# A step of four columns: from the turnings of the probabilities to the evictions of the keys

## The chip, the cores and the metric

The kernel runs on one core of a Trainium2 chip. The metric is the device time of one execution in microseconds, the median of several runs. The engines are TensorE (PE in the profile; PEld is its weight load), VectorE (DVE), ScalarE (ACT), GpSimd (POOL) and SyncE (SP), which here issues all DMAs.

## The reference, cut to what matters

32 graphs of 512 nodes with 512 features pass through two layers that share one adjacency matrix. The first is a graph attention with one head; the second is an attention with eight heads of 64 columns. Each layer adds its input and normalises.

```python
x = _layernorm(x + _L0_gnn_ref(x, adj, W, a))      # e = leaky(self + neighbour); masked softmax; alpha @ h; concat h
x = _layernorm(x + _L1_gnn_ref(x, adj, Wq, ...))
# inside the second:
scores = einsum('bhqd,bhkd->bhqk', q, k) / 8       # 512 x 512 for each of 8 heads
scores = where(adj == 0, -inf, scores)
attn = softmax(scores, axis=-1)
out = einsum('bhqk,bhkd->bhqd', attn, v)
```

## The kernel before

All of it is float32, and each matmul operand is split into a high and a low part (HI and LO, both float32r); a product is the sum of three matmuls (or two for the probabilities). The high part is written by ScalarE as a copy from PSUM, the low part by VectorE as the difference of PSUM and the high part, or by GpSimd where the source lies in SBUF.

Work is pipelined over graphs. One round handles the second attention of graph k, the first attention and the projections of graph k+1, and the loads of graph k+2. For each engine a plan (TENSOR_PLAN, SCALAR_PLAN, VECTOR_PLAN, GPSIMD_PLAN, SP_PLAN) writes out by hand in which order its pieces of a round are issued; engines meet at semaphores only, and each works in the order of its plan. The last graph has plans of its own, and a prologue comes ahead of the first.

The second attention of a graph has 32 steps s, one for each pair of a head and a tile of 128 queries:

- TensorE multiplies q and k of a pair of heads into one of four banks S_bank (line 791). Before that, q and k of the pair (two heads, 128 rows, 512 tokens) are evicted from R_bank into qk_pair with the bias added: high parts on ScalarE (line 848), low parts on VectorE (line 999), for q first and then for k, four pairs per graph.
- VectorE adds the mask to the scores while it writes them into prob (three slots) and takes the row extremum (reduce_scores, line 1082). The mask is bf16, 128 rows by 512 columns for each of four tiles.
- ScalarE takes the exponential in place, with the row sum (line 924).
- VectorE turns prob in blocks of 32 by 32 into blocked (turn_blocks, line 1102). The key of column c*128 + i*4 + d has to land in row i*4 + d of block column c later on, and so the turning reads the tile with a step of four columns: for a fixed c and d, 32 columns i that lie four apart.
- Four turned steps go to a scratch in HBM and come back with keys on the rows (scratch, then turned_lo_prob), as one store and one load.
- ScalarE makes the high part (line 838), GpSimd the low part (line 1161), and TensorE weighs v with both into O_bank (line 810).

The first attention of a graph runs its 512 by 512 coefficients through alpha, one tile of 128 rows at a time: ScalarE writes them (line 881), VectorE adds the mask and reduces in place (line 1027, four per graph), ScalarE takes the exponential, and TensorE turns alpha by transposes. Its columns are in the order of the nodes. The same mask serves both attentions.

The mask is built once at the start: adj is loaded into tokens[2], VectorE turns it into 0 or a huge negative number (line 1141), and SyncE waits for that (mask_built) before it loads WqT into the same place.

Of the kernel before, what the change touches and what calls it, by code (L numbers as in the profile page):

```python
# [21 lines left out]
ALU = mybir.AluOpType  # L22
ACT = mybir.ActivationFunctionType
F32 = mybir.dt.float32
F32R = mybir.dt.float32r
BF16 = mybir.dt.bfloat16
I32 = mybir.dt.int32

P = 128
BLK = 32  # L30
# [3 lines left out]
MASKED = -3.0e38  # L34
HUGE = 3.0e38
HI, LO = 0, 1
# [359 lines left out]
def graph_layers(nc, x, xT, adj, W, a, WqT, bq, WkT, bk, WvT, bv, WoT, bo, out):  # L396
    B, N, D = x.shape
    F1 = W.shape[1]
    T = N // P
# [8 lines left out]
    with ExitStack() as ctx:  # L408
# [6 lines left out]
        def sem(name):  # L415
# [8 lines left out]
        mask = sb("mask", [P, T, N], BF16)  # L424
# [5 lines left out]
        tokens = [sb(f"tokens{i}", [P, T, D]) for i in range(3)]  # L430
# [6 lines left out]
        a_negmax, a_sum, a_rsum = a_cols[:, 0, :], a_cols[:, 1, :], a_cols[:, 2, :]  # L437
# [5 lines left out]
        qk_pair = sb("qk_pair", [P, 4, N], F32R)  # L443
# [31 lines left out]
        ident_built, mask_built = sem("ident_built"), sem("mask_built")  # L475
# [7 lines left out]
        a_pre, a_red, a_exp, a_inv = sem("a_pre"), sem("a_red"), sem("a_exp"), sem("a_inv")  # L483
# [4 lines left out]
        qk_hi = sem("qk_hi")  # L488
        v_hi = sem("v_hi")
        s_mm, s_red, p_exp, p_inv, p_turned = (sem("s_mm"), sem("s_red"), sem("p_exp"), sem("p_inv"),  # L490
                                               sem("p_turned"))
# [13 lines left out]
        prologue = Round(0, -1, FIRST_LAYER, last=False)  # L505
        end = Round(0, B, END, more=False, load=False)

        def pair_bank(R, kind, pair):

            if (kind, pair) == ("q", 1):  # L510
                return R_bank[1 - R.bank("k1")]
            return R_bank[R.bank(f"{kind}{pair}")]
# [69 lines left out]
        def prob_tile(R, s):  # L582

            return prob[:, slot_of(R, s), :]
# [17 lines left out]
        def _(sp):  # L602
# [74 lines left out]
                load_tokens(start, i)  # L677
            for j, w in enumerate((WqT, WkT, WvT, WoT)):
                if j == 0:
                    sp.wait_ge(mask_built, 2)  # L680
                else:
                    sp.wait_ge(w_lo, j)
                place = tokens[2][:, :, :] if j % 2 == 0 else stage().rearrange("p (c n) -> p c n", c=C)
                sp.dma_start(place, w.rearrange("(c p) n -> p c n", p=P)).then_inc(w_loaded[1 + j], 16)
                if j == 1:
                    for i in range(T):
                        load_turned(prologue, i)
# [148 lines left out]
        def _(act):  # L836
# [3 lines left out]
            def qk_of_pair_hi(R, pair):  # L840

                if due(R.n(32, 8 * pair)):
                    act.wait_ge(s_mm, R.n(32, 8 * pair))
                for kind, b_col, dst in (("q", bq_col, 0), ("k", bk_col, 2)):

                    ring_mm_value = R.ring("k1") if (kind, pair) == ("q", 1) else R.ring(f"{kind}{pair}", 1)
                    act.wait_ge(ring_mm, ring_mm_value)
                    act.activation(qk_pair[:, dst + HI, :], pair_bank(R, kind, pair)[:, :], ACT.Identity,
                                   bias=b_col[:, pair % 4:pair % 4 + 1]).then_inc(qk_hi, 1)

            def layer_apply(R, which, ahead, i, done):
                t_ap = tokens[R.buffer(ahead)][:, i, :]
# [126 lines left out]
        def _(dve):  # L979
# [16 lines left out]
            def qk_of_pair_lo(R, pair):  # L996
                for j, (kind, b_col, dst) in enumerate((("q", bq_col, 0), ("k", bk_col, 2))):
                    dve.wait_ge(qk_hi, R.n(8, 2 * pair + j + 1))
                    dve.scalar_tensor_tensor(out=qk_pair[:, dst + LO, :], in0=pair_bank(R, kind, pair)[:, :],  # L999
                                             scalar=b_col[:, pair % 4:pair % 4 + 1],  # L1000
                                             in1=qk_pair[:, dst + HI, :].bitcast(F32), op0=ALU.add,
                                             op1=ALU.subtract).then_inc(ring_done, 1)

            def solo_hi_count(R, name):
# [4 lines left out]
            def piece(R, kind, i):  # L1009
# [14 lines left out]
                if kind == "red":  # L1024
                    al = alpha_of(R, i)
                    dve.wait_ge(a_pre, R.nx(4, i + 1))
                    dve.tensor_tensor_reduce(al, al, mask[:, i, :], -1.0, HUGE, ALU.add, ALU.min,  # L1027
                                             a_negmax[:, i:i + 1]).then_inc(a_red, 1)
                if kind == "evD":
                    out_name, t_ap = f"D{i}", tokens[R.buffer(1)][:, i, 0:F1]  # L1030
                    dve.wait_ge(a_inv, R.nx(4, i + 1))
# [63 lines left out]
            def turn_blocks(R, s):  # L1095
                ph = s // 4
                if s % 4 == 0 and due(R.n(8, ph - 1)):
                    dve.wait_ge(*stored(R, ph - 2))
                if s % 4 == 3 and due(R.n(16, 2 * ph - 2)):
                    dve.wait_ge(pv_mm, R.n(16, 2 * ph - 2))  # L1100
                dve.wait_ge(p_exp, R.n(32, s + 1))
                dve.transpose(blocked[:, ph % 2, :, :, 2 * (s % 2) + s % 4 // 2, :].rearrange("p d c i -> p c d i"),  # L1102
                              prob_tile(R, s).rearrange("p (c i d) -> p c d i", c=T, i=BLK)).then_inc(p_turned, 1)

            def half_sum(R, u):
                for w in range(2):
# [25 lines left out]
            for j in range(2):  # L1132
                for c in range(C):
                    if j + c > 0:
# [3 lines left out]
            dve.wait_ge(w_hi, 1)  # L1138
            split_lo(w0[:, LO, :, :], w_stage(), w0[:, HI, :, :], w_lo)
            dve.wait_ge(adj_loaded, 16)  # L1140
            dve.tensor_scalar(mask[:, :, :], tokens[2][:, :, :].bitcast(I32), 0.0, MASKED, ALU.is_equal,
                              ALU.mult).then_inc(mask_built, 1)
            dve.wait_ge(small_loaded, SMALL)
            run_round(start, [START])
            run_round(prologue, [PROLOGUE])
# [108 lines left out]
```

## Time and profile before

| what | value |
|---|---|
| median of 3 runs | 3222.71 us (3222.53 to 3223.19) |
| the profiled execution | 3226.84 us |
| its span, first to last instruction | 3225.0 us |
| mean granted TensorE clock | 0.987 |
| busy: TensorE, VectorE, ScalarE, GpSimd | 3002.1, 2969.1, 2460.1, 2020.8 us |

The span leaves out 1.84 us of the profiled execution's time. Busy time is the union of an engine's instructions; TensorE's matmuls are pipelined, and the ends of their records are modelled. A wait is put down to the semaphore that came last. The granted clock is a share of 2.4 GHz.

### The profile page before, as it was taken

How to read it: one execution, taken by the hardware profiler on the slowest of the kernel's cores; microseconds unless marked ns; L12 is line 12 of the kernel's file. 1: busy time of each engine (PE TensorE's matmuls, PEld its weight loads, DVE VectorE, ACT ScalarE, POOL GpSimd, SP SyncE). 2: the span in 40 equal slices, each digit the busy share in tenths (PEclk: the TensorE clock that was granted, in tenths of full speed). 3: DMA queues.
4: the chain of work that ended last, by engine and by line, in shares of the span. 5: the costliest groups of instructions: out<-in, count | busy, mean ns of one | idle time of the engine just before them, and what ended most of it. 6: DMA issues, size and time to landing. Idle time of an engine off the chain costs nothing.

```text
span 3225.0 us, 58281 instructions
## 1 busy us (share of the span) xinstructions
PE 3002.1 (93%) x19084; PEld 2506.7 (78%) x19084; DVE 2969.1 (92%) x6553; ACT 2460.1 (76%) x5031; POOL 2020.8 (63%) x1415
## 2 busy tenths in 40 slices
PE   5899999999999999999999999999999999999985
PEld 4787788777887787887787887887787877787874
DVE  4999999999999999999999999999999999999985
ACT  3777787777787777877777877777887777877764
POOL 1566666666666666666666666666666666666664
PEclk7999999999999999999999999999999999999998
DMA  3566666665665666666666666666666666666554
GB/s 121 193 211 215 222 235 213 215 210 207 235 226 210 214 214 216 225 233 210 214 213 219 224 228 210 215 215 214 223 230 212 215 213 219 225 217 214 203 199 154
DMA packets 306413, 685.39 MB, mean 213 GB/s; under 512 B 56896, under 2 KB 90432, under 8 KB 273344
## 3 DMA queue, kind: packets, MB, share of 16 engines
q1 hardware_dynamic: 306112, 681.68, 61.8%
q8 instruction: 153, 2.51, 0.3%
q14 instruction: 148, 1.21, 0.1%
HBM read 375.40 MB, written 306.18 MB: 211 GB/s over the span
## 4 chain that ended last, share of the span: by engine, by line
DVE 52%; PE 19%; issue 13%; ACT 7%; DMA 4%; POOL 2%; SPq 1%; DVEq 0%; ACTq 0%; POOLq 0%
DVE blocked L1102 22%; PE R_bank L721 11%; DVE prob L1082 8%; DVE stats L985 4%; DVE alpha L1027 4%; PE O_bank L810 4%; DVE qk_pair L999 3%; DVE o_half L1110 3%; PE S_bank L791 2%; ACT prob L924 2%; DVE tokens L1070 1%; PE L_bank L712 1%; DMA turned_lo_prob<-scratch 1%; DMA r_scratch<-r_cols 1%; ACT turned_hi_prob L838 1%
## 5 line engine op out<-in xcount | busy, mean ns | idle before, releaser
L1161 POOL TENSOR_TENSOR turned_lo_prob<-turned_lo_prob,turned_hi_prob 128x1024 fp32r<-128x1024 f32 x512 | 1237.3, 2433 | 587.3 <-ACT turned_hi_prob L838 585.9
L1102 DVE STREAM_TRANSPOSE blocked<-prob 128x512 f32<-128x512 f32 x1024 | 1102.3, 1099 | 42.6 <-ACT prob L924 30.9
L924 ACT ACTIVATE prob<-prob,small_cols 128x512 f32<-128x512 f32 x1024 | 736.0, 720 | 311.3 <-DVE small_cols L1082 305.4
L1082 DVE CUSTOM_DVE_ANT_0 prob<-S_bank,mask 128x512 f32<-128x512 f32 x1024 | 677.7, 681 | 6.9 <-PE S_bank L791 2.3
L810 PE MATMUL O_bank<-turned_hi_prob,v_st 128*128 128x256 f32 x2048 | 522.8, 292 | 70.2 <-POOL turned_lo_prob L1161 67.2
L838 ACT ACTIVATE turned_hi_prob<-turned_lo_prob 128x1024 fp32r<-128x1024 f32 x512 | 529.0, 1052 | 58.2 <-PE O_bank L810 32.9
L810 PE MATMUL O_bank<-turned_lo_prob,v_st 128*128 128x256 f32 x2048 | 508.3, 285 | 0.0
L810 PEld LDWEIGHTS O_bank<-turned_hi_prob,v_st 128*128 128x128 f32 x2048 | 394.6, 193 | 116.3 <-POOL turned_lo_prob L1161 99.8
L791 PE MATMUL S_bank<-qk_pair 64*128 64x512 f32 x3072 | 448.8, 417 | 31.8 <-DVE qk_pair L999 22.0
L721 PE MATMUL R_bank<-wv,x1T 128*128 128x256 f32 x3072 | 409.6, 287 | 2.2 <-DVE v_st L981 0.2
L721 PEld LDWEIGHTS R_bank<-wv,x1T 128*128 128x128 f32 x3072 | 380.6, 190 | 32.0 <-issue 23.0
L810 PEld LDWEIGHTS O_bank<-turned_lo_prob,v_st 128*128 128x128 f32 x2048 | 395.4, 193 | 4.1
L721 PE MATMUL R_bank<-x1T,wq 128*128 128x512 f32 x1536 | 385.3, 399 | 14.3 <-DVE v_st L981 14.3
L721 PE MATMUL R_bank<-wo,oT 128*128 128x512 f32 x1536 | 387.4, 401 | 2.9 <-POOL oT L1175 1.4
L721 PE MATMUL R_bank<-x1T,wk 128*128 128x512 f32 x1536 | 380.1, 396 | 0.2 <-DVE v_st L981 0.2
L791 PEld LDWEIGHTS S_bank<-qk_pair 64*128 64x128 f32 x3072 | 264.2, 186 | 142.3 <-DVE small_cols L1082 49.4
L721 PEld LDWEIGHTS R_bank<-x1T,wq 128*128 128x128 f32 x1536 | 279.8, 188 | 86.5 <-issue 27.5
L721 PEld LDWEIGHTS R_bank<-wo,oT 128*128 128x128 f32 x1536 | 279.5, 188 | 86.2 <-POOL oT L1175 16.5
L721 PEld LDWEIGHTS R_bank<-x1T,wk 128*128 128x128 f32 x1536 | 286.8, 188 | 68.9 <-DVE tokens L1070 1.0
L1155 POOL TENSOR_TENSOR o_half<-o_half,r_wide 128x256 f32<-128x256 f32 x256 | 189.2, 739 | 231.6 <-DVE o_half L1110 204.8
L1175 POOL TENSOR_TENSOR oT<-o_half,oT 128x256 fp32r<-128x256 f32 x256 | 189.7, 741 | 154.3 <-ACT oT L838 154.3
L1110 DVE TENSOR_TENSOR o_half<-O_bank,o_half 64x256 f32<-64x256 f32 x512 | 210.0, 410 | 47.2 <-ACT o_half L943 39.2
(90 smaller groups left out, 4364.4 us busy)
## 6 DMA issues: line engine op xcount, KB each, us to landing
scratch<-blocked SPq DMA_DIRECT2D x256, 1024.0 KB, 4.1
turned_lo_prob<-scratch SPq DMA_DIRECT2D x256, 1024.0 KB, 5.6
tokens<-xT SPq DMA_DIRECT2D x128, 256.0 KB, 4.8
tokens<-x SPq DMA_DIRECT2D x128, 256.0 KB, 3.6
r_wide<-r_scratch SPq DMA_DIRECT2D x512, 64.0 KB, 3.7
out<-tokens SPq DMA_DIRECT2D x128, 256.0 KB, 4.0
r_scratch<-r_cols SPq DMA_DIRECT2D x256, 16.0 KB
tokens<-adj SPq DMA_DIRECT2D x1, 1024.0 KB, 5.8
```

Source lines behind the costliest of these rows:

```text
L721: last = pe.matmul(dst, stationary(s, c), moving(m, c), start=(c, s, m) == todo[0], stop=(c, s, m) == todo[-1])
L791: last = pe.matmul(score_bank(R, 2 * u + w)[:, :], qk_pair[own, qp, t * P:(t + 1) * P], qk_pair[own, 2 + kp, :], start=j == 0, stop=j == 2)
L810: last = pe.matmul(O_bank[:, o_cols(w)], v_st[:, c, (2 * (ph // 2) + w) % HEADS, :], probs, start=(c, s) == todo[0], stop=(c, s) == todo[-1])
L838: act.activation(dst, src, ACT.Copy).then_inc(done, 1)
L924: act.activation(prob_tile(R, s), prob_tile(R, s), ACT.Exp, bias=negmax[:, slot:slot + 1], scale=-1.0, accum_out=psum_row[:, ph % 2, j:j + ...
L985: dve.bn_stats(stats[which][:, i % 2, :], t_ap).then_inc(ln_dve[which], 1)
L1082: dve.tensor_tensor_reduce(prob_tile(R, s), score_bank(R, s)[:, :], mask[:, s % 8 // 2, :], -SCALE, HUGE, ALU.add, ALU.min, negmax[:, slot ...
L1102: dve.transpose(blocked[:, ph % 2, :, :, 2 * (s % 2) + s % 4 // 2, :].rearrange("p d c i -> p c d i"), prob_tile(R, s).rearrange("p (c i d ...
L1110: dve.tensor_tensor(o_ap, O_bank[0:DH, o_cols(w)].rearrange("p (a t i) -> p a t i", a=4, t=2), o_ap, ALU.add).then_inc(o_sum, 1)
L1155: pool.tensor_tensor(o_half[:, :], o_half[:, :], r_wide[:, :], ALU.mult).then_inc(o_normed, 1)
L1161: pool.tensor_tensor(lo_ap, lo_ap.bitcast(F32), turned_hi_prob[:, 2 * a:2 * a + 2, :, :].bitcast(F32), ALU.subtract).then_inc(p_lo, 1)
L1175: pool.tensor_tensor(oT[:, LO, u // 2 % 4, o_cols(u % 2)], o_half[:, :], oT[:, HI, u // 2 % 4, o_cols(u % 2)].bitcast(F32), ALU.subtract). ...
```

## The change

The keys are laid out in another order. Where ScalarE and VectorE evict k (not q), they read the bank in steps of four columns and write in order, so that key 4m + d stands in column d*128 + m of qk_pair. The scores, the probabilities and the mask have their columns in this order too. The turning then reads 32 adjoining columns for each c and d (position d*128 + c*32 + i) and writes what it wrote before. The mask is built in the new order by four instructions, one for each tile, which read adj in steps of four; SyncE waits for the last of them. The first attention still has its columns in the order of the nodes: its masked reduction reads alpha in order and the mask in steps, four elements that lie 128 apart, then the next four.

```diff
--- before.py
+++ after.py
@@ -505,6 +505,14 @@
         prologue = Round(0, -1, FIRST_LAYER, last=False)
         end = Round(0, B, END, more=False, load=False)
 
+        def turned_keys(columns):
+
+            return columns.rearrange("p (d m) -> p d m", d=4)
+
+        def by_key_place(columns):
+
+            return columns.rearrange("p (m d) -> p d m", d=4)
+
         def pair_bank(R, kind, pair):
 
             if (kind, pair) == ("q", 1):
@@ -677,7 +685,7 @@
                 load_tokens(start, i)
             for j, w in enumerate((WqT, WkT, WvT, WoT)):
                 if j == 0:
-                    sp.wait_ge(mask_built, 2)
+                    sp.wait_ge(mask_built, 1 + T)
                 else:
                     sp.wait_ge(w_lo, j)
                 place = tokens[2][:, :, :] if j % 2 == 0 else stage().rearrange("p (c n) -> p c n", c=C)
@@ -845,8 +853,10 @@
 
                     ring_mm_value = R.ring("k1") if (kind, pair) == ("q", 1) else R.ring(f"{kind}{pair}", 1)
                     act.wait_ge(ring_mm, ring_mm_value)
-                    act.activation(qk_pair[:, dst + HI, :], pair_bank(R, kind, pair)[:, :], ACT.Identity,
-                                   bias=b_col[:, pair % 4:pair % 4 + 1]).then_inc(qk_hi, 1)
+                    hi_ap, bank_ap = qk_pair[:, dst + HI, :], pair_bank(R, kind, pair)[:, :]
+                    if kind == "k":
+                        hi_ap, bank_ap = turned_keys(hi_ap), by_key_place(bank_ap)
+                    act.activation(hi_ap, bank_ap, ACT.Identity, bias=b_col[:, pair % 4:pair % 4 + 1]).then_inc(qk_hi, 1)
 
             def layer_apply(R, which, ahead, i, done):
                 t_ap = tokens[R.buffer(ahead)][:, i, :]
@@ -996,9 +1006,11 @@
             def qk_of_pair_lo(R, pair):
                 for j, (kind, b_col, dst) in enumerate((("q", bq_col, 0), ("k", bk_col, 2))):
                     dve.wait_ge(qk_hi, R.n(8, 2 * pair + j + 1))
-                    dve.scalar_tensor_tensor(out=qk_pair[:, dst + LO, :], in0=pair_bank(R, kind, pair)[:, :],
-                                             scalar=b_col[:, pair % 4:pair % 4 + 1],
-                                             in1=qk_pair[:, dst + HI, :].bitcast(F32), op0=ALU.add,
+                    lo_ap, hi_ap, bank_ap = qk_pair[:, dst + LO, :], qk_pair[:, dst + HI, :], pair_bank(R, kind, pair)[:, :]
+                    if kind == "k":
+                        lo_ap, hi_ap, bank_ap = turned_keys(lo_ap), turned_keys(hi_ap), by_key_place(bank_ap)
+                    dve.scalar_tensor_tensor(out=lo_ap, in0=bank_ap, scalar=b_col[:, pair % 4:pair % 4 + 1],
+                                             in1=hi_ap.bitcast(F32), op0=ALU.add,
                                              op1=ALU.subtract).then_inc(ring_done, 1)
 
             def solo_hi_count(R, name):
@@ -1024,8 +1036,9 @@
                 if kind == "red":
                     al = alpha_of(R, i)
                     dve.wait_ge(a_pre, R.nx(4, i + 1))
-                    dve.tensor_tensor_reduce(al, al, mask[:, i, :], -1.0, HUGE, ALU.add, ALU.min,
-                                             a_negmax[:, i:i + 1]).then_inc(a_red, 1)
+                    by_node = al.rearrange("p (m d) -> p m d", d=4)
+                    dve.tensor_tensor_reduce(by_node, by_node, mask[:, i, :].rearrange("p (d m) -> p m d", d=4),
+                                             -1.0, HUGE, ALU.add, ALU.min, a_negmax[:, i:i + 1]).then_inc(a_red, 1)
                 if kind == "evD":
                     out_name, t_ap = f"D{i}", tokens[R.buffer(1)][:, i, 0:F1]
                     dve.wait_ge(a_inv, R.nx(4, i + 1))
@@ -1100,7 +1113,7 @@
                     dve.wait_ge(pv_mm, R.n(16, 2 * ph - 2))
                 dve.wait_ge(p_exp, R.n(32, s + 1))
                 dve.transpose(blocked[:, ph % 2, :, :, 2 * (s % 2) + s % 4 // 2, :].rearrange("p d c i -> p c d i"),
-                              prob_tile(R, s).rearrange("p (c i d) -> p c d i", c=T, i=BLK)).then_inc(p_turned, 1)
+                              prob_tile(R, s).rearrange("p (d c i) -> p c d i", c=T, i=BLK)).then_inc(p_turned, 1)
 
             def half_sum(R, u):
                 for w in range(2):
@@ -1138,8 +1151,9 @@
             dve.wait_ge(w_hi, 1)
             split_lo(w0[:, LO, :, :], w_stage(), w0[:, HI, :, :], w_lo)
             dve.wait_ge(adj_loaded, 16)
-            dve.tensor_scalar(mask[:, :, :], tokens[2][:, :, :].bitcast(I32), 0.0, MASKED, ALU.is_equal,
-                              ALU.mult).then_inc(mask_built, 1)
+            for t in range(T):
+                dve.tensor_scalar(turned_keys(mask[:, t, :]), by_key_place(tokens[2][:, t, :].bitcast(I32)), 0.0, MASKED,
+                                  ALU.is_equal, ALU.mult).then_inc(mask_built, 1)
             dve.wait_ge(small_loaded, SMALL)
             run_round(start, [START])
             run_round(prologue, [PROLOGUE])
```

## Rows read from the trace of the kernel before

**Rows 1.** The page, part 1: busy time, share of the span and instructions of each engine.
```profile
PE 3002.1 (93%) x19084; PEld 2506.7 (78%) x19084; DVE 2969.1 (92%) x6553; ACT 2460.1 (76%) x5031; POOL 2020.8 (63%) x1415
```
**Rows 2.** Windows: stretch, length, busy us by engine, granted clock, DMA share, GB/s.
```profile
180.00:3100.00 2920.00, 2786.41 (x17851) 2326.36 (x17851) 2764.24 (x6116) 2294.78 (x4706) 1888.90 (x1317) 1.00 0.64 217
...
3160.00:3225.00 65.00, 30.27 (x136) 24.84 (x136) 26.13 (x56) 25.18 (x47) 27.06 (x20) 0.75 0.40 140
```
**Rows 3.** Line 885 from 1300 to 1700 us: ns min/median/max, first and last start.
```profile
L885 ACT ACTIVATE n_wide<-L_bank x4: 590/590/591, 1356.3 to 1647.5; 128x512 f32<-128x512 f32 x4
```
**Rows 4.** TensorE's waits, 200 to 3000 us: total us, times, longest us.
```profile
PE O_bank L810 <- POOL turned_lo_prob L1161: 38.0, 33, 1.4
PE R_bank L721 <- DVE qk_pair L999: 27.6, 29, 1.0
PE L_bank L712 <- DVE x1T L981: 20.9, 29, 0.7
PE S_bank L791 <- DVE qk_pair L999: 16.2, 29, 0.9
PE R_bank L721 <- DVE v_st L981: 12.1, 30, 0.4
```
**Rows 5.** Groups of instructions by form: busy us, mean ns | idle us before, releasers.
```profile
L1102 DVE STREAM_TRANSPOSE blocked<-prob 128x512 f32<-128x512 f32 x1024 | 1102.3, 1099 | 42.6 <-ACT prob L924 30.9 <-PE O_bank L810 8.6
...
L1082 DVE CUSTOM_DVE_ANT_0 prob<-S_bank,mask 128x512 f32<-128x512 f32 x1024 | 677.7, 681 | 6.9 <-PE S_bank L791 2.3 <-issue 0.3
...
L999 DVE SCALAR_TENSOR_TENSOR qk_pair<-R_bank,b_cols,qk_pair 128x512 fp32r<-128x512 f32 x256 | 176.8, 732 | 6.0 <-ACT qk_pair L848 5.9
...
L848 ACT ACTIVATE qk_pair<-R_bank,b_cols 128x512 fp32r<-128x512 f32 x256 | 166.0, 686 | 39.6 <-PE R_bank L721 37.2
...
L1027 DVE CUSTOM_DVE_ANT_0 alpha<-alpha,mask 128x512 f32<-128x512 f32 x124 | 127.4, 1027 | 0.0
...
L1093 DVE STREAM_TRANSPOSE r_cols<-r_cols 128x32 f32<-128x32 f32 x256 | 54.2, 212 | 8.8
```
**Rows 6.** The tile alpha, line 1027: ns min/median/max, first and last start.
```profile
L1027 DVE CUSTOM_DVE_ANT_0 alpha<-alpha,mask x124: 645/685/2055, 96.7 to 3048.7; 128x512 f32<-128x512 f32 x124
```
**Rows 7.** Timeline of VectorE in a middle round: start us, us, instruction.
```profile
1500.20 0.67 DVE L1082 CUSTOM_DVE_ANT_0 prob<-S_bank,mask 128x512 f32<-128x512 f32 x1
...
1500.80 0.68 DVE L1082 CUSTOM_DVE_ANT_0 prob<-S_bank,mask 128x512 f32<-128x512 f32 x1
...
1519.81 3.11 DVE L1102 STREAM_TRANSPOSE blocked<-prob 128x512 f32<-128x512 f32 x3
```
**Rows 8.** Timeline from 1506 to 1513 us, three engines, cut to two waits.
```profile
1506.68 2.11 DVE L1102 STREAM_TRANSPOSE blocked<-prob 128x512 f32<-128x512 f32 x2
...
1507.53 1.27 ACT L848 ACTIVATE qk_pair<-R_bank,b_cols 128x512 fp32r<-128x512 f32 x2
...
1509.03 1.37 DVE L999 SCALAR_TENSOR_TENSOR qk_pair<-R_bank,b_cols,qk_pair 128x512 fp32r<-128x512 f32 x2
...
1510.31 1.10 DVE L1102 STREAM_TRANSPOSE blocked<-prob 128x512 f32<-128x512 f32 x1
...
1510.45 0.96 PE L791 MATMUL S_bank<-qk_pair 64*128 64x512 f32 x6 [0.50 <-DVE qk_pair L999]
...
1511.35 0.64 DVE L981 TENSOR_TENSOR x1T<-L_bank,x1T 128x512 fp32r<-128x512 f32 x1
...
1512.14 0.63 PE L712 MATMUL L_bank<-ident,tokens 128*128 128x128 f32 x4 [0.72 <-DVE x1T L981]
```
**Rows 9.** Timeline of the start, 12 to 24 us.
```profile
13.34 2.29 DVE L1141 TENSOR_SCALAR mask<-tokens 128x2048 bf16<-128x2048 int32 x1
14.58 5.05 SPq L614 DMA_DIRECT2D tokens<-x  x4
...
18.14 0.42 DVE L981 TENSOR_TENSOR h<-S_bank,h 128x256 fp32r<-128x256 f32 x1 [2.50 <-ACT h L838]
```

## The prediction

> **What bounds the kernel now.** I began with the shares of the page [rows 1]: TensorE 93%, VectorE 92%, ScalarE 76%, GpSimd 63% of the span. An average hides the start and the end, so next the windows [rows 2]. Between 180 and 3100 us TensorE is busy 2786.4 of 2920 us (95.4%) and VectorE 2764.2 (94.7%), at a granted clock of 1.00, the 2.4 GHz level. Two engines are nearly full at once. The copy of the neighbours' terms, issued once per graph, starts at 1356.3 and, three rounds later, at 1647.5 [rows 3]: a round takes 97.07 us, in which TensorE is idle 4.6% = 4.4 us and VectorE works 91.9 us.
>
> A change that relieves VectorE can therefore win no more than TensorE's idle time, 2920 - 2786.4 = 133.6 us in this stretch, and the little beyond it that lies under overlapping tails of matmul records. Whose fault is that idle time? The waits of TensorE [rows 4] (200 to 3000 us) sum to 114.8 us: 76.8 us are charged to VectorE (qk_pair 27.6 and 16.2, x1T 20.9, v_st 12.1) and 38.0 to GpSimd's low part of the probabilities, which itself comes at the end of a path through VectorE's turnings.
>
> The timeline shows how [rows 8]. ScalarE has the high parts of q and k ready by 1508.80, but VectorE sits in two turnings from 1506.68 to 1508.79 and starts the low parts only at 1509.03, ending at 1510.40. TensorE's scores start at 1510.45 after 0.50 us of idling. The next turning, 1510.31 to 1511.41, stands ahead of x1T's low part, and TensorE idles 0.72 us for that one.
>
> **The change part by part.** *Turnings.* 1024 of them take 1099 ns each, 1102.3 us together [rows 5]. Other VectorE work on as many columns, the masked reduction of the scores, takes 681 ns. Back to back the prices are 1.00 us per turning (three in 3.11 us, one record 1.10) and 0.60 us per reduction (1500.20 to 1500.80) [rows 7]. What singles out the turning is its reading step of four columns and that it turns 32 by 32 blocks; the change removes the first and keeps the second. Lower bound of the saving: 0, if turning is what costs. Upper bound: 1.00 - 0.60 = 0.40 us each. A turning of 32 adjoining columns takes 212 ns [rows 5], near the small instructions' floor, so it tells only that (1099 - 212)/480 = 1.85 ns are paid per further column against 681/512 = 1.33 ns for a whole reduction, fixed part included. I take 0.40: 32 per round, 12.8 us of VectorE per round, 410 us in all.
>
> The rows leave open which of the two properties costs. The Trainium skill ("SBUF — State Buffer", Specifications (TRN2)) states that SBUF is read in lines of 16 bytes and wants at least two hits in a line for full bandwidth; a step of four 4-byte columns hits each line once. By it the whole 0.40 us is the step's and the sum is the one made here; without it the saving could be 0 and the result the second rival's. No run shows it yet.
>
> *Evictions of the keys.* Half of the 256 evictions on each engine, 128 on ScalarE (686 ns) and 128 on VectorE (732 ns) [rows 5], now read PSUM in steps of four columns; the VectorE one reads and writes SBUF in order. No row has such a read of PSUM. Bounds: nothing, and the step's price on the turnings, 1099 - 681 = 0.42 us; four keys a round, so 0 to 1.7 us a round on each engine. I take the middle, 0.8 us. The wait for the eviction's result is covered as long as VectorE is early: in [rows 8] 0.82 us of turnings vanish ahead of the low parts, about what both stepped evictions would add at worst.
>
> *First attention.* 128 reductions (1027 ns on average [rows 5], 645 at the least and 2055 at the most [rows 6]) read the mask in steps: 0 to 0.42 us each, 0 to 1.7 us a round. I take 1.7, since this step spans more bytes than the turnings' step. Net relief of VectorE per round: 12.8 - 0.8 - 1.7 = 10.3 us, so it falls from 91.9 to 81.6 us, clearly under TensorE's 92.6. ScalarE gains 0.8 us of work and has 21% free.
>
> *Mask.* One instruction of 2.29 us becomes four of 512 columns, 0.68 to 1.10 us each by the rows above, 2.7 to 4.4 us: 0.4 to 2.1 us later. VectorE then idles 2.50 us anyway, and SyncE, which now waits for the fifth count ahead of WqT, issues loads until 19.63 [rows 9]. Hidden, price nothing; if ScalarE's first h came sooner it would cost those 2.1 us once. In the prologue four stepped reductions may add 1 us. No DMA is added, and no queue is passed by another step.
>
> **The sum.** TensorE becomes the only full engine. How much of its 133.6 us comes back? The lower bound is nothing, the upper all. The scores' wait in [rows 8] goes entirely (0.82 us earlier against 0.50). The wait for x1T's low part goes only in part: the trip over ScalarE and VectorE between two transposes through one bank stays, although the turning ahead of it shrinks. The wait for GpSimd has its slack upstream, where GpSimd is busy 65% [rows 2]. So of five kinds of wait four should go or nearly go and one should stay, with something new in the gaps: I take two thirds, 89 us. The last graph has less for TensorE to do, and the stretch from 3160 us on is a chain, with TensorE busy 30 and VectorE 26 of 65 us [rows 2]: I count half of that graph's 32 turnings as lying in its way, 16 x 0.40 = 6 us, an estimate. The prologue takes 1 back. Sum: 94 us of the profiled execution's 3226.84 (span 3225.0 and 1.84 around it): 3132.8. The median of the runs is 4.1 lower, 3222.7, so I forecast **3129 us**, 2.9% faster.
>
> **Rivals.**
> *TensorE never waits.* If all 133.6 us and 10 at the end come back: 3222.7 - 144 = 3079; with the hidden tails perhaps 25 us less. For it: VectorE would have 15 us spare per round. Against: the orders on all engines are fixed, and the trip x1T makes is not VectorE's load. It decides if TensorE passes 99% busy.
>
> *The turning itself costs.* Then the turnings stay at 1.1 us and only costs are added: on VectorE, 94.7% full, 0 to 3.4 us a round (four evictions and four reductions at 0.42). Time: 3222.7 to 3222.7 + 31 x 3.4 = 3328, about 3275 with half of it. This is the case that ends slower; it decides if a turning saves less than an eighth of what one eviction and one first-attention reduction lose together, because there are 1024 against 128 and 128. For it: no row here reads adjoining columns in a long turning. Against: a step of reading is the one thing in which the turning's form is odd.
>
> *Stepped reads of PSUM are dear and exposed.* Each of the four keys per round would reach the scores later by twice 0.42 us, and dearer still if such a read costs more than a stepped read of SBUF. If half of 31 x 3.4 us shows, 52 us of the gain go: about 3181. For it: two of TensorE's waits are already on qk_pair [rows 4]. Against: the order leaves other matmuls between most keys and their scores. The Trainium skill ("PSUM — Partial Sum Buffer", Specifications (TRN2)) states lines of 8 bytes there and says that patterns which do not adjoin slow matmuls markedly; of evictions by ScalarE or VectorE it says nothing. By that rule carried over to evictions this rival's 3181 would be the time. No row of before shows it.
>
> *Relief without effect.* VectorE goes idle, but the fixed orders hand TensorE the same waits: a third of the idle time comes back, 45 + 5 us, 3173; with next to none, no change.
>
> **How the numbers follow.** A difference below 0.2% (6 us) is about what a measurement of this kernel can't tell from none. Chances: my forecast, 3090 to 3165, 0.58; TensorE never waits, under 3090, 0.10; dear evictions or relief with little effect, 3165 to 3216, 0.17; nothing left of it, within 0.2%, 0.06; the turning itself costs or the additions outweigh, 0.09. Faster 0.85, same 0.06, slower 0.09. The range 3070 to 3205 leaves out half of the second case's lower end, the last quarter of the third, and the last two: about 0.2.
>
> **What would show it.** In the profile after: turnings at 680 to 720 ns, some 420 us gone from their group; L848 and L999 split into two durations, or not, which prices the stepped read of PSUM; the first attention's reduction longer by up to 0.42 us at its shortest; VectorE near 87% and TensorE near 98% in the middle stretch, a round of about 94.1 us; TensorE's waits on qk_pair and v_st nearly gone, the one on x1T left. The forecast is wrong if the turnings keep 1.1 us, if TensorE's waits on qk_pair grow, or if ScalarE rather than TensorE becomes what others wait for.

## The result, and the profile after

The changed kernel takes 3136.2 us (median of 4 runs, 3133.3 to 3137.2) against 3222.6 us for the one before: a ratio of 0.973, interval 0.9718 to 0.9742. The forecast was 3129 us. The profiled execution took 3133.3 us, its span was 3131.5. Times here and below are medians of fast runs; one run below, of the kernel with the first attention in order and less work for TensorE, took 3168.2 us at a granted clock of 0.843 and is left out.

The page of the changed kernel, part 1, beside [rows 1]:

```profile
PE 2970.1 (95%) x19084; PEld 2504.4 (80%) x19084; DVE 2670.4 (85%) x6556; ACT 2445.5 (78%) x5031; POOL 2040.9 (65%) x1415
```

VectorE works 299 us less. TensorE, with the same 19084 matmuls, is busy 32 us less; that fewer of its pipelined tails lie bare ahead of a wait is a reading that no run here shows.

The middle stretch, beside [rows 2]: TensorE is busy 97.3% of it after 95.4%, VectorE 87.5% after 94.7%, as the prediction's signs had it.

```profile
180.00:3000.00 2820.00, 2743.41 (x17745) 2314.14 (x17744) 2467.94 (x6081) 2267.97 (x4680) 1898.47 (x1309) 1.00 0.65 224
```

The groups by form, busy us and mean ns, beside [rows 5] (lines have moved by 8 to 14):

```profile
L1115 DVE STREAM_TRANSPOSE blocked<-prob 128x512 f32<-128x512 f32 x1024 | 696.4, 697 | 113.9 <-PE O_bank L818 59.4 <-ACT prob L934 51.4
L1095 DVE CUSTOM_DVE_ANT_0 prob<-S_bank,mask 128x512 f32<-128x512 f32 x1024 | 678.3, 681 | 35.5 <-PE S_bank L799 31.2 <-issue 0.8
...
L1012 DVE SCALAR_TENSOR_TENSOR qk_pair<-R_bank,b_cols,qk_pair 128x512 fp32r<-128x512 f32 x256 | 181.6, 741 | 27.4 <-ACT qk_pair L859 21.8
...
L859 ACT ACTIVATE qk_pair<-R_bank,b_cols 128x512 fp32r<-128x512 f32 x256 | 168.6, 686 | 48.4 <-PE R_bank L729 44.3
...
L1040 DVE CUSTOM_DVE_ANT_1 alpha<-alpha,mask 128x512 f32<-128x512 f32 x124 | 192.7, 1554 | 13.2 <-ACT alpha L891 13.2
...
L1155 DVE TENSOR_SCALAR mask<-tokens 128x512 bf16<-128x512 int32 x4 | 6.6, 1712 | 0.0
```

The turnings fall from 1099 to 697 ns, 405.9 us in all. The evictions, half of which now read PSUM in steps, stay at 686 ns on ScalarE and go from 732 to 741 ns on VectorE. The first attention's reduction goes from 1027 to 1554 ns, 65.3 us more.

The copy of the neighbours' terms gives the round, beside [rows 3]: (1697.0 - 1318.9) / 4 = 94.5 us after 97.1.

```profile
L895 ACT ACTIVATE n_wide<-L_bank x5: 589/589/589, 1318.9 to 1697.0; 128x512 f32<-128x512 f32 x5
```

TensorE's waits from 200 to 2900 us, beside [rows 4]; the same stretch of the kernel before has 110.9 us, here it is 69.1:

```profile
PE R_bank L729 <- DVE qk_pair L1012: 27.5, 29, 1.3
PE L_bank L720 <- DVE x1T L991: 17.8, 29, 0.7
PE S_bank L799 <- DVE small_cols L1095: 12.4, 28, 0.5
PE O_bank L818 <- POOL turned_lo_prob L1175: 11.4, 28, 0.4
```

The scores' wait for qk_pair and the one for v_st are gone, GpSimd's is down to a third, x1T's is nearly as it was. But R_bank's wait for qk_pair has not moved, and the scores wait for a reduction instead. The timeline shows what stands ahead of the first of these:

```profile
1434.11 5.64 POOL L1175 TENSOR_TENSOR turned_lo_prob<-turned_lo_prob,turned_hi_prob 128x1024 fp32r<-128x1024 f32 x2 [6.80 <-ACT turned_hi_prob L846]
...
1435.15 2.33 DVE L1040 CUSTOM_DVE_ANT_1 alpha<-alpha,mask 128x512 f32<-128x512 f32 x1
...
1437.40 0.69 DVE L1095 CUSTOM_DVE_ANT_0 prob<-S_bank,mask 128x512 f32<-128x512 f32 x1
...
1438.13 0.72 ACT L934 ACTIVATE prob<-prob,small_cols 128x512 f32<-128x512 f32 x1 [1.36 <-DVE small_cols L1095]
...
1440.43 1.26 ACT L859 ACTIVATE qk_pair<-R_bank,b_cols 128x512 fp32r<-128x512 f32 x2
...
1441.15 1.41 DVE L1012 SCALAR_TENSOR_TENSOR qk_pair<-R_bank,b_cols,qk_pair 128x512 fp32r<-128x512 f32 x2 [0.39 <-ACT qk_pair L859]
...
1441.96 1.70 PE L729 MATMUL R_bank<-h,turned 128*128 128x256 f32 x12 [0.93 <-DVE qk_pair L1012]
```

Read it from below. TensorE waits 0.93 us for the low part of q, which frees the bank for its next matmuls, VectorE for ScalarE's high part, ScalarE had exponentials ahead of that and waited 1.36 us for a reduction on VectorE, and that stood behind the first attention's reduction, which took 2.33 us. The same chain stood in the kernel before, and the prediction, which followed the scores' wait and x1T's through the timeline, had not read it:

```profile
1477.05 1.13 DVE L1027 CUSTOM_DVE_ANT_0 alpha<-alpha,mask 128x512 f32<-128x512 f32 x1
...
1478.83 0.73 ACT L924 ACTIVATE prob<-prob,small_cols 128x512 f32<-128x512 f32 x1 [1.42 <-DVE small_cols L1082]
...
1482.66 1.70 PE L721 MATMUL R_bank<-h,turned 128*128 128x256 f32 x12 [0.96 <-DVE qk_pair L999]
```

The reduction of 2.33 us began during a GpSimd instruction; where none ran it is short, as at 1427.97, after GpSimd had ended at 1427.31:

```profile
1427.97 1.08 DVE L1040 CUSTOM_DVE_ANT_1 alpha<-alpha,mask 128x512 f32<-128x512 f32 x1
```

Over the whole trace, 33 of the 124 reductions began with no GpSimd instruction running and took 1066 to 1083 ns; in the kernel before these were 63, of 645 to 685 ns. All others ended a nearly fixed time after the GpSimd instruction during which they began, 0.92 to 0.98 us here (one 1.06) and 0.546 to 0.554 us before: such a reduction waits until that instruction has ended. So the step costs 0.40 to 0.42 us with GpSimd or without. 124 times 0.41 us are 51 of the 65.3; the rest are longer waits for GpSimd, during whose instructions 91 now begin instead of 61.

The Trainium skill ("GPSIMD Engine Reference", Key points) says that GpSimd shares its SBUF interfaces with VectorE and contends with VectorE instructions that have two inputs in SBUF. This reduction has two, the scores' one (681 ns in both kernels) has one in PSUM; the rows agree.

### The profile page after: what moved, and what is told of

It reads as the page before. It is cut to its first block, busy times and chain, and to the rows that moved or that the text cites. A ratio compares the mean times of both kernels' runs of the same rounds, so it can differ in the third digit from the quotient of the medians.

```text
span 3131.5 us, 58284 instructions
## 1 busy us (share of the span) xinstructions
PE 2970.1 (95%) x19084; PEld 2504.4 (80%) x19084; DVE 2670.4 (85%) x6556; ACT 2445.5 (78%) x5031; POOL 2040.9 (65%) x1415
## 4 chain that ended last, share of the span: by engine, by line
PE 71%; DVE 14%; issue 7%; ACT 5%; DMA 1%; POOL 1%; DVEq 0%; SPq 0%; ACTq 0%; POOLq 0%
PE R_bank L729 41%; PE O_bank L818 11%; PE S_bank L799 9%; PE L_bank L729 6%; PE L_bank L720 4%; DVE blocked L1115 3%; DVE stats L995 3%; DVE prob L1095 2%; DVE tokens L1083 2%; ACT qk_pair L859 1%; DVE o_half L1123 1%; DVE alpha L1040 1%; DVE x1T L991 1%; DVE qk_pair L1012 1%; ACT alpha L891 1%
## 5 line engine op out<-in xcount | busy, mean ns | idle before, releaser
L1175 POOL TENSOR_TENSOR turned_lo_prob<-turned_lo_prob,turned_hi_prob 128x1024 fp32r<-128x1024 f32 x512 | 1250.2, 2459 | 539.1 <-ACT turned_hi_prob L846 539.0
L1115 DVE STREAM_TRANSPOSE blocked<-prob 128x512 f32<-128x512 f32 x1024 | 696.4, 697 | 113.9 <-PE O_bank L818 59.4
L818 PE MATMUL O_bank<-turned_hi_prob,v_st 128*128 128x256 f32 x2048 | 521.7, 292 | 38.4 <-POOL turned_lo_prob L1175 38.3
L729 PE MATMUL R_bank<-wv,x1T 128*128 128x256 f32 x3072 | 401.3, 286 | 0.2
```

The lines of the kernel that those rows point to most:

```text
L729: last = pe.matmul(dst, stationary(s, c), moving(m, c), start=(c, s, m) == todo[0], stop=(c, s, m) == todo[-1])
L818: last = pe.matmul(O_bank[:, o_cols(w)], v_st[:, c, (2 * (ph // 2) + w) % HEADS, :], probs, start=(c, s) == todo[0], stop=(c, s) == todo[-1])
L1175: pool.tensor_tensor(lo_ap, lo_ap.bitcast(F32), turned_hi_prob[:, 2 * a:2 * a + 2, :, :].bitcast(F32), ALU.subtract).then_inc(p_lo, 1)
```

## The experiments

Two theories went in. *TensorE bounds*: after the change TensorE is the only full engine, so what is left of VectorE's additions costs little. *The additions took back gain*: the stepped first attention stands where TensorE waits. Later a third came up, that round trips in fixed orders pace the round. The kernel before was between 3221.6 and 3222.9 us beside these runs.

**The step by itself.** The kernel before, with four reading steps side by side, for the turnings, the evictions, the first attention and the mask, run once and read for its durations:

```diff
+                if s % 4 == 0:
+                    dve.transpose(turned_to, src.rearrange("p (x i) -> p x i", i=BLK)).then_inc(p_turned, 1)
+                elif s % 4 == 1:
+                    dve.transpose(turned_to.rearrange("p (x e) i -> p x e i", e=2),
+                                  src.rearrange("p (x i e) -> p x e i", i=BLK, e=2)).then_inc(p_turned, 1)
...
```

> The kernel before, with the reading step varied inside one run; the columns' order is left wrong by it. Turnings read in steps of 1, 2, 4 and 8 columns (4, 8, 16, 32 bytes) by s modulo 4; evictions of k in steps of 1, 2, 4, 8 by pair; the first attention's mask in steps of 1, 2, 4 and 16 columns (2, 4, 8, 32 bytes) by tile; the mask built in steps of 1, 2, 4, 8, one tile each. Theory: a step of 16 bytes or more in SBUF costs, one of 8 does not: turnings 0.70, 0.70, 1.10, 1.10 us; first attention at its shortest 0.65, 0.65, 0.65, 1.07 us; evictions 0.69 and 0.74 us at every step, since PSUM charges nothing. Rival one: the price grows with the step, so 0.70, 0.85, 1.10, over 1.2 us. Rival two: any step but 1 costs the same 1.10 us. The mask's build, 1.72 us a tile in the changed kernel, should be 0.69 us at steps 1 and 2 and 1.7 us at 4 and 8 by the theory.

Turnings at steps of 1, 2, 4 and 8 columns, ns min/median/max:

```profile
L1143 DVE STREAM_TRANSPOSE blocked<-prob x256: 656/704/739, 81.9 to 3098.6; 128x512 f32<-128x512 f32 x128
L1145 DVE STREAM_TRANSPOSE blocked<-prob x256: 667/702/724, 82.7 to 3100.4; 128x512 f32<-128x512 f32 x128
L1148 DVE STREAM_TRANSPOSE blocked<-prob x256: 1054/1080/1131, 85.9 to 3101.0; 128x512 f32<-128x512 f32 x128
L1151 DVE STREAM_TRANSPOSE blocked<-prob x256: 1093/1200/1259, 87.1 to 3105.0; 128x512 f32<-128x512 f32 x128
```

A step of 8 bytes is free, 16 bytes cost 0.38 us and 32 bytes 0.50 us. The price jumps between 8 and 16, as the theory has it, and grows a little more after. Evictions of k at a step of 8 columns, first ScalarE, then VectorE, cost what those of k cost in order in the kernel before (medians of 682 and 742 ns):

```profile
L864 ACT ACTIVATE qk_pair<-R_bank,b_cols x32: 677/680/691, 143.4 to 3079.4; 128x512 fp32r<-128x512 f32 x32
L1028 DVE SCALAR_TENSOR_TENSOR qk_pair<-R_bank,b_cols,qk_pair x32: 739/742/744, 144.5 to 3082.1; 128x512 fp32r<-128x512 f32 x32
```

The mask as an operand (bf16, read in steps of 2, 4 and 16 columns, that is 4, 8 and 32 bytes; in the prologue, one of each) and as an output (from steps of 1, 2, 4 and 8 of int32):

```profile
L1059 DVE CUSTOM_DVE_ANT_1 prob<-prob,mask x1: 679/679/679, 33.2 to 33.2; 128x512 f32<-128x512 f32 x1
L1062 DVE CUSTOM_DVE_ANT_1 prob<-prob,mask x1: 682/682/682, 33.8 to 33.8; 128x512 f32<-128x512 f32 x1
L1065 DVE CUSTOM_DVE_ANT_1 prob<-prob,mask x1: 1091/1091/1091, 36.1 to 36.1; 128x512 f32<-128x512 f32 x1
...
L1190 DVE TENSOR_SCALAR mask<-tokens x1: 656/656/656, 13.8 to 13.8; 128x512 bf16<-128x512 int32 x1
L1192 DVE TENSOR_SCALAR mask<-tokens x1: 1496/1496/1496, 14.4 to 14.4; 128x512 bf16<-128x512 int32 x1
L1194 DVE TENSOR_SCALAR mask<-tokens x1: 1717/1717/1717, 15.8 to 15.8; 128x512 bf16<-128x512 int32 x1
L1196 DVE TENSOR_SCALAR mask<-tokens x1: 1778/1778/1778, 17.5 to 17.5; 128x512 bf16<-128x512 int32 x1
```

The operand is free up to 8 bytes as well. The reduction of the remaining tile, in order, began during a GpSimd instruction and took 1756 ns, so 645 to 685 ns from the kernel before stand for it.

The mask's build takes 1.50 us already at a step of 8 bytes, but that isn't the step's price. Each of the four began during a GpSimd instruction and ended soon after it, some 0.3 us after at 4 and 8 bytes and some 0.5 us after at 16 and 32. Two of these GpSimd instructions, beside the steps of 8 and of 32 bytes, and the builds of a later run (the changed kernel with its first attention in order), of which one with the changed kernel's 16-byte step took 0.62 us:

```profile
14.18 1.46 POOL L1236 TENSOR_TENSOR x1T<-tokens,x1T 128x512 fp32r<-128x512 f32 x1
...
17.02 1.70 POOL L1236 TENSOR_TENSOR x1T<-tokens,x1T 128x512 fp32r<-128x512 f32 x1
...
L1154 DVE TENSOR_SCALAR mask<-tokens x4: 615/1699/1748, 13.4 to 18.3; 128x512 bf16<-128x512 int32 x4
```

**The turnings alone.** One line of the change put into the kernel before:

```diff
-                              prob_tile(R, s).rearrange("p (c i d) -> p c d i", c=T, i=BLK)).then_inc(p_turned, 1)
+                              prob_tile(R, s).rearrange("p (d c i) -> p c d i", c=T, i=BLK)).then_inc(p_turned, 1)
```

> The kernel before with the turnings alone reading in order, and nothing done about the order of the keys (probabilities meet the wrong keys). No stepped eviction, no stepped first attention, no four-part mask. Theory (TensorE is the bound after, the additions cost little): 3115 to 3136 us, at most 0.7% under the changed kernel. Rival (the additions took back much of the gain): 3080 to 3105 us.

3096.7 us, ratio 0.961 (0.9595 to 0.9624): 125 us off where the whole change takes off 86. The rival holds: the additions took back 39 us.

**Which addition.** The changed kernel with one of them undone:

```diff
-                    by_node = al.rearrange("p (m d) -> p m d", d=4)
-                    dve.tensor_tensor_reduce(by_node, by_node, mask[:, i, :].rearrange("p (d m) -> p m d", d=4),
+                    dve.tensor_tensor_reduce(al, al, mask[:, i, :],
```

> The changed kernel, but the first attention reads the mask in order (so its mask is in the wrong order). VectorE loses 4 x 0.53 = 2.1 us a round. Theory (TensorE is the bound): 3125 to 3136 us. Rival (the longer reduction stands ahead of the evictions that TensorE still waits 0.95 us a round for): those waits go, 3136 - 28 = about 3108 us.

3097.3 us, 0.9613 (0.9599 to 0.9628). All 39 us were the first attention's; the stepped evictions and the mask's build cost nothing that shows, since this kernel has them and the one before has not. TensorE's waits, same stretch, 38.4 us in place of 69.1:

```profile
PE L_bank L720 <- DVE x1T L991: 17.9, 29, 0.7
PE O_bank L818 <- POOL turned_lo_prob L1174: 12.6, 30, 0.4
PE R_bank L729 <- DVE qk_pair L1012: 7.9, 29, 0.6
```

The wait on qk_pair falls from 27.5 to 7.9 and the one on the reduction of the scores is gone.

**The same addition to the kernel before.** The mirror image of that diff.

> The kernel before, but the first attention reads the mask in the steps of the changed kernel (so its mask is in the wrong order): 2.1 us of VectorE more per round, where VectorE is 94.7% full. Theory (both engines bound the kernel before, and each waits for the other): about +60 us, 3283. Rival (TensorE alone was the bound): 0 to +15 us, up to 3238.

3274.2 us, 1.016 (1.0143 to 1.0177): 52 us slower, for 49 us more in the group of these reductions (127.4 to 176.8). In the kernel before, a microsecond put on VectorE at this place was a microsecond of time; no other place was tried.

**Less work for TensorE.** Sixteen matmuls of 512 columns per round left out, in both kernels:

```diff
-                            lambda m, c: wo[:, m, c, :], ring_mm, R.n(8, 0) if i == 0 else None)
+                            lambda m, c: wo[:, m, c, :], ring_mm, R.n(8, 0) if i == 0 else None, PARTS[0::2])
```

> The kernel before, with the output projection made of two of its three products (high by high and low by high; the low part of Wo is left out): 16 matmuls of 512 columns fewer per round, 16 x 0.233 = 3.7 us of TensorE per round, 119 us in all. Theory (VectorE was as full as TensorE): most of it is lost in waits for VectorE, 0 to -45 us, 3178 to 3223. Rival (TensorE alone was the bound): -100 to -119 us, about 3110.

> The changed kernel with the same products left out: 119 us of TensorE fewer. Theory (TensorE is now the only bound): -80 to -119 us, 3017 to 3056. Rival (fixed orders and round trips between engines set the pace, not TensorE's work): 0 to -45 us, 3091 to 3136.

Before: 3218.4 us, 0.9985 (0.9976 to 0.9995), 4 us for 119 us of work. TensorE's work didn't bound the kernel before; most of it came back as waits (110.9 to 191.8 us from 200 to 2900 us). The most of these are put down to ScalarE's exponentials of the first attention and to GpSimd, so that VectorE bound this kernel rests on the addition above and not on this run. After: 3154.4 us, which is 18 us *slower* than with the work. The theory's second half falls. TensorE's waits grew from 69.1 to 147.3 us; the longest three of this kernel:

```profile
PE O_bank L818 <- POOL turned_lo_prob L1175: 58.4, 87, 1.3
PE R_bank L729 <- DVE qk_pair L1012: 28.4, 29, 1.3
PE R_bank L729 <- POOL oT L1189: 20.5, 28, 0.7
```

and its mean granted clock fell from 0.988 to 0.976:

```profile
core 0: 3147.0 us, clock 0.976
```

The trace has rounds at either level of the clock. From 110 to 778 us it is 1.00; from there on one stretch in most rounds is at 0.50, the 1.2 GHz level, each time about the second of two waits of TensorE. The first:

```profile
775.68 0.39 PE L818 MATMUL O_bank<-turned_hi_prob,v_st 128*128 128x256 f32 x1 [1.30 <-POOL turned_lo_prob L1175]
...
777.87 2.71 PE L729 MATMUL R_bank<-h,turned 128*128 128x256 f32 x12 [0.97 <-DVE qk_pair L1012]
...
778.20:781.50 3.30, 3.30 (x18) 3.30 (x17) 1.64 (x5) 1.63 (x6) 0.00 (x0) 0.50 0.31 113
```

The same two waits stand in the rounds ahead, where the clock did not fall; why it fell from there on stays open. The rounds, first of the changed kernel, then of this one at the upper level and with such stretches:

```profile
L895 ACT ACTIVATE n_wide<-L_bank x6: 588/589/591, 277.8 to 750.9; 128x512 f32<-128x512 f32 x6
L895 ACT ACTIVATE n_wide<-L_bank x6: 590/590/591, 278.3 to 749.8; 128x512 f32<-128x512 f32 x6
L895 ACT ACTIVATE n_wide<-L_bank x5: 590/591/591, 1323.7 to 1705.8; 128x512 f32<-128x512 f32 x5
```

That is 94.6, 94.3 and 95.5 us a round. At the upper level the work left out gives 0.3 us a round, some 9 us for 119; the 20 rounds with a stretch at 1.2 GHz lose 1.2 us each, 24 us. The difference of 15 is that of the profiled executions (3148.8 to 3133.3). So even without the lower clock the work hardly counts.

**A kernel faster than both.** Two masks of bytes in the room of one of bf16, one in each order, so that after the start no turning and no reduction on VectorE reads SBUF in steps:

```diff
-        mask = sb("mask", [P, T, N], BF16)
+        mask = sb("mask", [P, T, N], F8)
+        node_mask = sb("node_mask", [P, T, N], F8)
...
+            dve.tensor_scalar(node_mask[:, :, :], tokens[2][:, :, :].bitcast(I32), 0.0, ALLOWED, ALU.not_equal, ALU.mult)
+            for t in range(T):
+                dve.tensor_copy(turned_keys(mask[:, t, :]), by_key_place(node_mask[:, t, :]))
```

> The changed kernel with two masks of bytes (255 where an edge is, 0 elsewhere, added to the scores, which the softmax takes out again; an entry without an edge is left with a weight e^-32 of its score's) in the room of the one bf16 mask: one in the order of the nodes for the first attention, one in the order of the keys. The second is copied from the first in steps of four bytes. No part of the attention reads in steps any more. Theory (the stepped first attention costs the changed kernel 39 us): 3090 to 3103 us. Rival (byte operands are slow in the masked reduction): reductions over 0.75 us each and 3136 us or more.

3100.1 us, 0.9623 (0.9609 to 0.9636). The masked reduction of the scores stays at 681 ns on average with bytes. The gain of the turnings is kept and the first attention's loss avoided. It rests on scores whose gap within a row stays well under 255.

**Where TensorE's work could pay.** First with the first attention out of the way (its reduction reading in order, as above), then in another part of the round:

```diff
-                            ring_mm)
+                            ring_mm, None, PARTS[0::2] if i >= 3 else PARTS)
```

> The changed kernel with the first attention reading in order (wrong mask order) and, as in the run before, the output projection in two of three products, which takes 3.7 us of TensorE per round out of its first third. Theory A (that stretch is paced by the first attention's path over VectorE and ScalarE, and the step lengthened it): with the step gone TensorE's relief pays there at last, 3097 - 30 to -80 us. Theory B (round trips of the probabilities over HBM, ScalarE and GpSimd pace that stretch): it pays under 20 us, 3077 to 3105.

> The changed kernel with the projections of q and k of pairs 3 and 4 in two of three products (low part of the weights left out): again 16 matmuls of 512 columns, 3.7 us of TensorE per round, but from the later two thirds of the round. Theory (TensorE's work does bound those thirds): -60 to -115 us against the changed kernel, 3021 to 3076. Rival (nowhere does TensorE's work alone bound): under 25 us, 3111 or more.

3092.3 us, 0.9599 (0.9584 to 0.9614), 5 us under the kernel that it starts from: theory B. And 3121.1 us, 0.9686 (0.9673 to 0.9699), 15 us for 119 us of work: the rival. In the second, TensorE's waits sum to 149.7 us, 80.6 more than in the changed kernel; the two that lead:

```profile
PE O_bank L818 <- POOL turned_lo_prob L1175: 52.5, 57, 2.0
PE R_bank L729 <- DVE qk_pair L1012: 27.5, 29, 1.3
```

**A fence moved.** From the two byte masks on, the wait that guards turned_lo_prob goes from VectorE to SyncE; then both reliefs of TensorE on top.

```diff
-                if s % 4 == 3 and due(R.n(16, 2 * ph - 2)):
-                    dve.wait_ge(pv_mm, R.n(16, 2 * ph - 2))
...
                 sp.wait_ge(*stored(R, ph))
+                if due(R.n(16, 2 * ph - 2)):
+                    sp.wait_ge(pv_mm, R.n(16, 2 * ph - 2))
```

> The kernel with two byte masks, and one wait moved: that the weighing of two phases earlier has read turned_lo_prob is awaited by SyncE ahead of the load into it, and no longer by VectorE ahead of every second... of each phase's last turning. The two-deep ring of the probabilities (turning, store, load, high part, low part, weighing) loses the turning and the store, some 5 us, from its loop. Theory C (that ring paces the round, and neither TensorE's nor VectorE's work does): 15 us or more under the kernel with two byte masks, 3085 or less. Rival D (the ring has slack; VectorE's 46 us of waits there are only shifted): 3095 to 3105, with those 46 us gone from VectorE's waits on O_bank and standing elsewhere.

> The same, with both reliefs of TensorE at once (output projection, and q and k of pairs 3 and 4, in two of three products): 7.5 us of TensorE fewer per round, 238 us in all, so that TensorE works 84 us of a round. Theory C with TensorE as the next bound: 2900 to 2990. Rival D (trips between the engines in their fixed orders pace every part of the round): 3050 to 3100; ScalarE's and VectorE's busy shares would tell whether one of them is then full.

3080.6 us (3076.6 to 3091.1), 0.9557 (0.954 to 0.9574), the fastest kernel here that leaves nothing out: 20 us under the byte masks, and the 46 us of VectorE's waits on O_bank ahead of turnings are gone, as rival D had it. The time is theory C's, so that loop was one of the things that set the pace. Again as rival D has it, VectorE waits longer elsewhere in the same stretch (for the scores 26.8 to 45.2 us, for h 41.7 to 61.0), and the gain can't be read from TensorE's waits: in the profiled execution, the slowest of the four, they sum to 41.3 us, with byte masks alone to 41.0.

```profile
DVE blocked L1115 <- PE O_bank L819: 46.5, 113, 0.5
```

But with 238 us less for TensorE it is 3053.5 us, 0.9475 (0.9458 to 0.9492): 27 us, rival D's number. No engine is full there: from 180 to 2900 us TensorE is busy 93%, VectorE 87%, ScalarE 82%.

```profile
180.00:2900.00 2720.00, 2526.58 (x16636) 2107.29 (x16635) 2379.11 (x6019) 2229.38 (x4627) 1851.35 (x1294) 1.00 0.67 230
```

**Load or place.** As much VectorE time as the step costs, taken from the layer statistics of the changed kernel:

```diff
-                dve.bn_stats(stats[which][:, i % 2, :], t_ap).then_inc(ln_dve[which], 1)
+                dve.bn_stats(stats[which][:, i % 2, :], t_ap[:, 0:F1]).then_inc(ln_dve[which], 1)
```

> The changed kernel with the layer statistics taken over half the columns (256 of 512; the norm is then of half a row): 8 instructions per round shorter by about 0.27 us, 2.1 us of VectorE per round, as much as the stepped reading cost the first attention, but taken at other places. If VectorE's load still sets the changed kernel's pace: 30 to 60 us off, 3076 to 3106. If it is the place of the first attention's reduction, ahead of the evictions that TensorE waits for, and not the load: over 3120.

3113.8 us, 0.9662 (0.9646 to 0.9678): 22 us, between the two expectations, for 68.3 us less in that group (172.5 to 104.2). The wait on qk_pair went to 7.9 us here too, because some of these statistics stand in the same stretch of VectorE's order, ahead of the evictions; the scores' wait for the reduction stayed, at 14.5 us. Reading in order took 61.2 us off the first attention's group (192.7 to 131.5) and gave 39, so the place counts. That load counts besides isn't excluded, since this load was partly in the place.

## Why the prediction was right, and where its reason was not

- *VectorE bounds the kernel before along with TensorE*: right for VectorE as far as one place shows it (52 us for 49 us added), wrong for TensorE (4 us for 119 us taken away). Two engines at 95% weren't two bounds.
- *The turnings' step*: 0.40 us each was forecast, 0.402 measured, and the ladder shows that it is the step and not the turning. The rule of 16-byte lines that the prediction weighed, the Trainium skill's ("SBUF — State Buffer", Specifications (TRN2)), agrees: 0.70 us at 8 bytes, 1.08 at 16.
- *Evictions*: 0.8 us a round was taken from the middle of the bounds; it is nothing, on either engine: those of k alone have medians of 682 ns on ScalarE and 742 ns on VectorE in both kernels. The 9 ns more in VectorE's mean are those of q, which read in order, and the kernel with the turnings alone changed has them too. The rival that held stepped PSUM reads dear is refuted.
- *First attention*: the term of the sum that was mis-sized. 1.7 us a round was taken, 2.1 measured: the step adds 0.42 us to the shortest of them (645 to 1066 ns), as the bound said, and 0.53 us on average, with the longer waits for GpSimd, for which the sum had no term. More than the size, the place was missed: I priced it as load on an engine with room and didn't name what is queued behind it. It held up ScalarE's exponentials, the evictions behind these, and TensorE.
- *Mask*: 6.6 us in place of 2.7 to 4.4. VectorE began the first low part at 20.10 us, after 18.14 before. The excess is waiting for GpSimd and not the step. Hidden all the same: the kernel with the stepped build and the one without it are 0.6 us apart.
- *Which waits go*: four of five kinds should nearly go. Three did (scores on qk_pair, v_st, most of GpSimd's), x1T stayed as forecast, R_bank's on qk_pair stayed against it, and one on the scores' reduction came in. The forecast had followed the scores' wait and x1T's through the timeline and took R_bank's, the longest of VectorE's, to go with the scores'; ahead of it stood the first attention's reduction, which the change made longer.
- *The sum*: 94 us forecast, 93.5 measured on the profiled executions (3226.8 to 3133.3), 86 on the medians. That the two meet is partly luck. Two thirds of TensorE's idle time, 89 us, should have come back; over the whole span it fell from 222.9 to 161.4 us (span less busy time), by 61.5, and in the middle stretch from 4.6% to 2.7%. The other 32.0 us are busy time, for which the sum had nothing. And what was missed on either side made up for each other: without the first attention's step it would have been 125 us, between the 94 forecast and the 144 of the first rival.
- *TensorE becomes the only full engine*: this step failed as a statement on what bounds. Where TensorE's work stays the same, time is that work and its waits, so fewer waits show in full: 30.7 us fewer in 2700 went with 39 us, 17.2 fewer with 22. Work that is taken from it doesn't pay, as four kernels show; it turns into waits for GpSimd's low parts and for qk_pair, of half a microsecond to one on average. That it is these trips in their fixed orders, and not one engine, that set the round after is the reading that fits all runs; it is shown as far as two of them go, since shortening them (the first attention's reduction, the fence) paid 39 and 20 us. Which trip is next wasn't tried.

## What to carry to other kernels

A reading step may be moved from many instructions to few, and where it lands counts: in reads of PSUM by ScalarE and VectorE it was free here, in a second SBUF operand it cost 0.4 us per 512 columns from 32 bytes on, with the wait for GpSimd on top. When a change adds time to an instruction on an engine that it also relieves, look at what is queued behind that instruction before calling it hidden. An engine that is busy 97% isn't shown to be the bound until taking work from it shortens the time.

## What the runs showed of the hardware that was not expected

Stepped reads of PSUM at 16 and 32 bytes cost neither ScalarE (680 ns) nor VectorE (742 ns) anything.

A VectorE reduction with two operands in SBUF that begins during a GpSimd instruction ends a fixed time after it, 0.55 us in order and 0.95 us with the step; the long reductions here are waits. The mask's build, with one operand in SBUF, was held up likewise. In the one case where it took 0.62 us, the GpSimd instruction beside it took 2.24 us, where the three ahead of it had taken 1.65 to 1.69.

With the output projection shortened, TensorE's granted clock fell to 1.2 GHz for a stretch of most rounds, and the kernel became slower than with the work. With as many matmuls left out in another part of the round the mean stayed at 0.988.
